# Products with the rounded activation issued on ScalarE's signal, those with the remainder on VectorE's, in a two-layer decoder on one Trainium2 core

## The reference, cut to what matters

```python
# layer 0: gated mixer, cross attention over 77 context rows, mixture of experts
xz = x @ W_in.T; xb, z = split(xz)
xc = silu(causal_conv4(xb));  proj = xc @ W_xproj.T          # B (16), C (16), delta (512)
y = (softplus(delta) * xc * sum(B * C) + D * xc) * silu(z);  mix = y @ W_out.T
att = softmax((x @ Wq) (ctx @ Wk).T / 8) (ctx @ Wv) @ Wo + bo # 16 heads of 64
moe = shared(x) + sum over the top 2 of 8 experts
# layer 1: self attention with rotary embedding (16 heads of 16), the same cross attention,
#          attention over tokens that a likeness with g_info picks
qkv = x @ W_qkv.T; att = softmax(q k.T / 4) v @ W_out.T
```

## Time and profile before

| | us |
|---|---|
| timed runs | 1549.1 and 1558.88, median 1553.99 |
| profiled execution | 1544.36 |
| its span, first to last instruction | 1542.3 |
| PE busy | 1326.4 (86%) |
| DVE busy | 979.2 (63%) |
| ACT busy | 650.5 (42%) |
| POOL busy | 423.6 (27%) |
| mean granted clock of TensorE | 0.932 of full |

### The profile page before, as it was taken

The page is one execution under the profiler, slowest core; times in us unless marked ns, Lnnn a source line. Parts: engine busy times, 40 slices in busy tenths (PEclk is TensorE's granted clock), DMA queues, the critical chain, the costliest instruction groups (busy, mean ns, idle before and its releaser), DMA issues.

```text
span 1542.3 us, 27793 instructions
## 1 busy us (share of the span) xinstructions
PE 1326.4 (86%) x11854; PEld 1097.8 (71%) x11854; DVE 979.2 (63%) x1785; ACT 650.5 (42%) x806; POOL 423.6 (27%) x405
## 2 busy tenths in 40 slices
PE   6899899998999999997699779878977957888785
PEld 6788788888878889996377558737755855556553
DVE  3676767767676446777675836666583656566573
ACT  6554556445543435652343245233414531432413
POOL 5131030210422744675034412702430240000000
PEclk9999999999999999999899899979989976978989
DMA  9361210111050316873002100200100030110000
GB/s 288 136 225 34 47 34 8 41 34 49 1 225 28 106 46 201 277 248 94 1 1 71 32 1 17 79 8 1 47 29 1 1 123 6 38 56 15 1 16 14
DMA packets 46138, 103.33 MB, mean 67 GB/s; under 512 B 4336, under 2 KB 26480, under 8 KB 45120
## 3 DMA queue, kind: packets, MB, share of 16 engines
q1 hardware_dynamic: 42944, 93.18, 18.4%
q0 software_dynamic: 3072, 8.39, 1.7%
HBM read 64.79 MB, written 36.77 MB: 66 GB/s over the span
## 4 chain that ended last, share of the span: by engine, by line
PE 68%; DVE 20%; ACT 6%; issue 3%; POOL 2%; DMA 1%; SPq 0%; POOLq 0%; DVEq 0%; ACTq 0%
PE ps L115 13%; PE ps L116 12%; PE ps L117 12%; DVE sm L1776 9%; PE ps L798 9%; PE ps L1217 4%; PE ps L1223 4%; PE ps L971 4%; PE ps L955 3%; ACT m L1639 2%; DVE m L1765 2%; DVE r L1765 2%; PE ps L1198 2%; DVE m L2192 1%; PE ps L1331 1%
## 5 line engine op out<-in xcount | busy, mean ns | idle before, releaser
L1391 ACT ACTIVATE m<-ps 128x1024 f32<-128x1024 f32 (+4 forms) x208 | 166.4, 813 | 324.7 <-PE ps L117 163.9
L1776 DVE TENSOR_REDUCE sm<-ps 128x8 f32<-128x2048 f32 (+1 forms) x128 | 193.0, 1532 | 59.0 <-PE ps L1198 34.3
L2420 POOL TENSOR_SCALAR sm<-sm 128x2 f32<-128x2 f32 x40 | 8.7, 218 | 724.1 <-DVE sm L1794 724.1
L1765 DVE TENSOR_TENSOR r<-ps,r 128x512 fp32r<-128x512 f32 (+1 forms) x159 | 116.2, 737 | 130.3 <-ACT r L1391 129.4
L1391 ACT ACTIVATE r<-ps 128x512 fp32r<-128x512 f32 (+1 forms) x159 | 100.8, 640 | 216.0 <-PE ps L798 113.6
L1639 ACT ACTIVATE m<-ps 128x2048 f32<-128x2048 f32 x64 | 119.6, 1877 | 169.2 <-PE ps L1217 169.2
L798 PE MATMUL ps<-cst,m 128*77 128x128 f32 (+1 forms) x1024 | 136.5, 277 | 21.6 <-DVE m L1765 9.4
L798 PEld LDWEIGHTS ps<-cst,m 128*77 128x77 f32 (+1 forms) x1024 | 115.0, 146 | 45.8 <-issue 17.1
L115 PE MATMUL ps<-r,w0h 128*128 128x256 f32 (+1 forms) x416 | 122.2, 294 | 16.8 <-DVE r L1765 12.5
L1198 PE MATMUL ps<-m 32*128 32x256 f32 x1024 | 103.4, 538 | 33.9 <-DVE sm L1776 30.7
L116 PE MATMUL ps<-r,w0h 128*128 128x256 f32 (+1 forms) x416 | 120.7, 290 | 0.0
(11 more groups left out here) (304 smaller groups left out, 3559.1 us busy)
## 6 DMA issues: line engine op xcount, KB each, us to landing
raw<-wu_dram SPq DMA_DIRECT2D x20, 768.0 KB, 5.6
keep_dram<-m SPq DMA_DIRECT2D x8, 768.0 KB, 3.5
m<-keep_dram SPq DMA_DIRECT2D x8, 768.0 KB, 4.3
xs_dram<-gsq SPq DMA_DIRECT2D x2, 2944.0 KB, 17.7
ys_dram<-m SPq DMA_DIRECT2D x23, 256.0 KB, 2.5
room<-wu_dram SPq DMA_DIRECT2D x7, 768.0 KB, 4.9
rt<-xs_dram SPq DMA_DIRECT2D x16, 256.0 KB, 3.2
w1raw<-w_dram SPq DMA_DIRECT2D x1, 3840.0 KB, 11.7
```

Of the source, the lines that this page charges most:

```text
L1391: return act.activation(o, i, ACT.Copy)
L1765: return dve.tensor_tensor(o, a, b_, op)
L1776: return dve.tensor_reduce(o, i, AX.X, op, **kw)
```

## The change

Two pairs of helpers split `mm3`. `whole` and `rest` are for stationary weights and a moving activation: `whole` issues the two products with the activation's rounded half, `rest` the one with the remainder. `whole_l` and `rest_l` are for a stationary activation. Each projection of a split activation waits for ScalarE's signal, issues products of `whole`, waits for VectorE's and issues those of `rest`. Where two output chunks share a bank, only one of them (chunks 0 and 2) is treated so, and the other two follow with `mm3`. The cross attention's transposed input now goes to bank 3, since its first query products, into banks 0 and 1, no longer wait for VectorE's reading of that bank. The mixer's output projection, which writes bank 2, gets a wait for VectorE's copy of the key and value products that stood there (`kv_ev[1]`). In the last sublayer `project_out` gets VectorE's signal for both. The experts keep `mm3`.

```diff
+def whole(pe, o, w, r, start):
+    pe.matmul(o, w[0], r[0], start=start, stop=False)
+    return pe.matmul(o, w[1], r[0], start=False, stop=False)
+
+def rest(pe, o, w, r, stop):
+    return pe.matmul(o, w[0], r[1], start=False, stop=stop)
+
+def whole_l(pe, o, l, w, start):
+    pe.matmul(o, l[0], w[0], start=start, stop=False)
+    return pe.matmul(o, l[0], w[1], start=False, stop=False)
+
+def rest_l(pe, o, l, w, stop):
+    return pe.matmul(o, l[1], w[0], start=False, stop=stop)
...
+                pe.wait_ge(*st.l0_act.at(b, "xT"))
+                pe.wait_ge(*w0_lo_v.at("win"))
...
+                for c in (0, 2):
+                    for k in range(2):
+                        whole(pe, into[c][0], into[c][1][k], cols(xT, A, k), k == 0)
                 pe.wait_ge(*st.l0_dve.at(b, "xT"))
...
+                for c in (0, 2):
                     for k in range(2):
-                        m = mm3(pe, st.ps[:, 1024 + c * 256:1280 + c * 256], cols(v.win, A, k, slice(c * 128, (c + 1) * 128)), cols(xT, A, k), k == 0, k == 1)
+                        rest(pe, into[c][0], into[c][1][k], cols(xT, A, k), k == 1)
+                yield
+                for c in (1, 3):
+                    for k in range(2):
+                        m = mm3(pe, into[c][0], into[c][1][k], cols(xT, A, k), k == 0, k == 1)
...
+                if 1 < b < 6:
+                    pe.wait_ge(*kv_ev[1].at(b - 2, 3))
+                for h in range(2):
+                    pe.wait_ge(*st.l0_act.at(b, f"y{h}"))
+                    for j in range(2):
+                        for k in (2 * h, 2 * h + 1):
+                            whole_l(pe, bank(st, 2 + j)[:, 0:256], cols(v.yr, A, k, slice(j * 128, (j + 1) * 128)), cols(v.wout, A, k), k == 0)
...
-                turn_x(st, b, sig)
-                yield
-                pe.wait_ge(*dve_.at(b, "xT"))
+                turn_x(st, b, sig, bank(st, 3))
+                yield
+                pe.wait_ge(*act_.at(b, "xT"))
...
                     if c % 2 == 0:
+                        pe.wait_ge(*act_.at(b, f"o{c // 2}"))
+                        for d in (c, c + 1):
+                            for j in range(2):
+                                whole_l(pe, bank(st, j)[:, 0:256], cols(v.OT, A, d, slice(j * 128, (j + 1) * 128)), cols(v.wo, A, d), d == 0)
+                    else:
                         pe.wait_ge(*dve_.at(b, f"o{c // 2}"))
...
-            def project_out(st, b, v, w, sig, dve_, o):
-                pe.wait_ge(*dve_.at(b, "oT"))
+            def project_out(st, b, v, w, sig, rounded, left, o):
+                pe.wait_ge(*rounded)
                 for j in range(2):
                     for c in range(2):
-                        m = mm3(pe, o[:, j * 256:(j + 1) * 256], cols(v.oT, A, c, slice(j * 128, (j + 1) * 128)), cols(w, A, c), c == 0, c == 1)
+                        whole_l(pe, o[:, j * 256:(j + 1) * 256], cols(v.oT, A, c, slice(j * 128, (j + 1) * 128)), cols(w, A, c), c == 0)
+                    if j == 0:
+                        pe.wait_ge(*left)
+                    for c in range(2):
+                        m = rest_l(pe, o[:, j * 256:(j + 1) * 256], cols(v.oT, A, c, slice(j * 128, (j + 1) * 128)), cols(w, A, c), c == 1)
...
-                yield from project_out(st, b, v, wfp, sig, dve_, bank(st, 2))
+                yield from project_out(st, b, v, wfp, sig, dve_.at(b, "oT"), dve_.at(b, "oT"), bank(st, 2))
```

Besides, the eleven tables of turns have other numbers, for instance:

```diff
-    "POOL": [3, 3, 3, 5, 12, 12, 12, 13, 13, 13, 13, 13, 16, 17, 18, 21, 21],
+    "POOL": [1, 4, 5, 8, 9, 11, 13, 13, 13, 13, 13, 13, 15, 16, 16, 16, 16],
```

More of the change, by code:

```diff
@@ L873, in l0 @@
                     if k % 2 == 0:
+                        pe.wait_ge(*st.l0_act.at(b, f"xr{k // 2}"))
+                    whole(pe, st.ps[0:48, 0:256], cols(v.wxp, A, k, slice(0, 48)), cols(v.xr, A, k), k == 0)
+                for k in range(4):
+                    if k % 2 == 0:
                         pe.wait_ge(*st.l0_dve.at(b, f"xr{k // 2}"))
-                    m = mm3(pe, st.ps[0:48, 0:256], cols(v.wxp, A, k, slice(0, 48)), cols(v.xr, A, k), k == 0, k == 3)
+                    m = rest(pe, st.ps[0:48, 0:256], cols(v.wxp, A, k, slice(0, 48)), cols(v.xr, A, k), k == 3)
                 m.then_inc(sig.up(b, "pB"), 1)
@@ L937, in xattn @@
                         yield
-                    for c in range(4):
-                        if c == 2:
-                            yield
+                    into = [(pair(st, i)[:, c * 256:(c + 1) * 256], [cols(v.wq, A, k, slice((4 * i + c) * 128, (4 * i + c + 1) * 128)) for k in range(2)]) for c in range(4)]
+                    for c in (0, 2):
                         for k in range(2):
-                            m = mm3(pe, pair(st, i)[:, c * 256:(c + 1) * 256], cols(v.wq, A, k, slice((4 * i + c) * 128, (4 * i + c + 1) * 128)), cols(xT, A, k), k == 0, k == 1)
+                            whole(pe, into[c][0], into[c][1][k], cols(xT, A, k), k == 0)
+                    if i == 0:
+                        pe.wait_ge(*dve_.at(b, "xT"))
+                    for c in (0, 2):
+                        for k in range(2):
+                            rest(pe, into[c][0], into[c][1][k], cols(xT, A, k), k == 1)
+                    yield
+                    for c in (1, 3):
+                        for k in range(2):
+                            m = mm3(pe, into[c][0], into[c][1][k], cols(xT, A, k), k == 0, k == 1)
                     m.then_inc(sig.up(b, f"q{i}"), 1)
@@ L1252, in a1 @@
                     pe.wait_ge(*r_dve.at("y", NT - 1))
-                yield from qkv(st, b, wao, sig, dve_, st.q_act if b >= 2 else None)
+                yield from qkv(st, b, wao, sig, act_, dve_, st.q_act if b >= 2 else None)
                 yield
@@ L1478, in xattn @@
                 act.wait_ge(*mix_dve.at(b, "ln"))
-                turned_x(st, b, xT_of(st, 3 if L else 1)[0], pe_, sig)
+                turned_x(st, b, xT_of(st, 3 if L else 1)[0], pe_, sig, bank(st, 3))
                 yield
@@ L1916, in xattn @@
                 yield
-                turned_x(st, b, xT_of(st, 3 if L else 1), act_, sig)
+                turned_x(st, b, xT_of(st, 3 if L else 1), act_, sig, bank(st, 3))
                 yield
```

46 lines of the change are left out of this document (23 added, 23 removed).

## The result

| | before | after |
|---|---|---|
| timed runs, us | 1549.1, 1558.88 | 1529.43, 1536.05 |
| median | 1553.99 | 1532.74 |
| span of the profiled execution | 1542.3 | 1534.1 |
| mean granted clock there | 0.932 | 0.921 |

The ratio is 0.9844, with a 95% interval of 0.9805 to 0.9883: 1.6% faster, inside the 2% band. The effect is real: 21 us in the first runs, 23 and 25 in the repeats.

A forecast was written before the change was run, and what follows sets the result against it. TensorE was taken to bound most of the kernel, with 28.1 us of its waits for VectorE's remainder touchable. Terms 8.8 + 3.4 + 3.8 + 1.0 = 17.0, plus 3 for the clock: 1549.1 - 20 = 1529 us, range 1507 to 1554.

The forecast's parts named there:

- One wait: A projection's first product starts on ScalarE's signal, saving 0.72 us; eight products cover VectorE's remainder.
- Layer 0, 8.8 us: Layer 0's 14 waits for VectorE's remainder, 13.6 us idle: seven save 0.72 us each, shorter ones go whole; 8.8 us.
- Queries, keys and values, 3.4 us: Layer 1's ten such waits: 0.9 us for each of three later pairs, VectorE being late next, plus 0.7; 3.4 us.
- Output projection, 3.8 us: Layer 1's output projections: eight waits save 0.47 us each, the time of four products issued ahead; 3.8 us.
- Swaps of the tables, 1.0 us: Layer 1: score block moved ahead of the transposes, and its like in cross attention; 0.2 us at 8 places, rounded to 1.
- The clock, 3 us: Layer 0: shorter stops bring fewer half-speed stretches; half of 7 us taken, less 0.5 for stretches elsewhere; 3 us.
- all three stretches named: Layer 0's half-clock stretches, behind 240.57 and near 278 and 377 us, 14 us in all, at waits the change shortens.
- All comes through (1516): Rival: the 28.1 us of idle go whole, plus 5 us of the clock's 7; 33 us, time 1516; chance 0.22.
- VectorE takes over (1541): Rival: VectorE and the layer norm replace the removed waits; 8 us gained, none from the clock, time 1541; chance 0.22.
- The second stop or load of weights (1559): Rival: each of 144 further TensorE waits costs a weight load, 27 us; net 7 to 10 slower, 1559; chance 0.08.
- Moved turns give it back (1544): Rival: moved turns in layers 0 and 1 return 12 us, with no clock gain; time 1544; chance 0.12.
- What would show it: Profile signs: remainder waits below 20 us, ScalarE's 10 to 15, layer 0 shorter by 8 to 12, layer 1 by 7 to 9.

The follow-up runs named there:

- E5: The changed kernel unaltered, run again beside the kernel before: median 1524.41 us, ratio .9851.
- E12: The changed kernel unaltered, run a third time beside the kernel before: median 1523.43 us, ratio .9852.
- E8: The changed kernel, but every projection in layer 0 waits for VectorE's signal first, leaving early starts in layer 1 only: 1538.15 us, ratio .9938.
- E4: The changed kernel with order, extra waits and tables kept, but products with the rounded half also wait for VectorE's signal: 1536.00 us, ratio .9941.
- E9: The changed kernel, but in layer 0 only the projections of x start early; those of xr, yr and OT wait for VectorE: 1526.46 us, ratio .9862.
- E7: The changed kernel, but every projection in layer 1 waits for VectorE's signal first, leaving early starts in layer 0 only: 1529.87 us, ratio .9874.
- E1: The kernel before with all eleven new tables of turns and no early starts: 1538.22 us, ratio .9952.
- E2: The changed kernel with the eleven old tables, so early starts without the new tables: 1528.34 us, ratio .9868.
- E10: The changed kernel, with the last sublayer's output projection also starting on ScalarE's signal and writing bank 3: 1520.97 us, ratio .9843.
- E3: The changed kernel with the old LAST table alone: 1519.38 us, ratio .9829.
- E6: The changed kernel with the old LAST table alone, repeated in a later job: 1522.89 us, ratio .9838.

## Why the prediction was right

The forecast was 1529 with 1507 to 1554, the measurement 1532.74, and 1523 to 1524 in the repeats. As a difference, 20 us were forecast, and 21 (first runs) to 25 (last job) measured. The largest term, layer 0, was right. The swaps of the tables were booked 3.9 us too low and the clock 3 too high; that these two cancelled is luck.

**One wait.** 0.72 us for a start on ScalarE's signal and eight products as enough cover: both as measured (1.89 to 1.17; no wait at `rest`).

**Layer 0, 8.8 us.** Right. The stage is 14.6 shorter. Its half-clock time fell from 24 to 10 us. Between E5 and E12, one kernel, 7 us of half clock in layer 0 cost 3.2 us (424.9 against 428.1); over all eight profiles with the changed layer 0 (six with 10 us, two with 17) they cost 2.6. So 14 us are worth 5 to 6 and the starts themselves 8 to 9. At one clock E8 gives 9.4. E4 and E8, without these starts, lose all of it, and E9 shows that the projections of x have most of it, as the earlier trace rows had it. One reading was off: six of the 14 waits have 1.4 to 1.9 us of idle time, not seven; the one counted as the seventh has 0.77, so the sum stands.

**Queries, keys and values, 3.4 us.** The size was too small. From the end of the layer norm behind one pair's self attention to the last ScalarE copy of the next pair's queries, where no half clock falls, there are 74.2 us before, 73.7 with the tables alone, 72.1 in the kernel after: 1.6 us for each of three pairs by the signals, where 0.9 was booked, 4.8 in sum. The step that failed is "what is late next is VectorE itself: 0.5 and 0.4 us". The remainder's waits of layer 1 do stand, shorter, at L135 (three, 0.5 us each: the four products of 512 columns don't reach over a remainder that starts late). But in the pair of the earlier trace rows TensorE's last transpose ends 20.8 us behind the layer norm instead of 22.6, while VectorE's last rotation ends only 0.9 earlier. The transposes follow TensorE's products without a stop in both, and now start (849.81) 1.6 us ahead of that rotation's end: it isn't on the path of everything behind.

**Output projection, 3.8 us.** Right. A pair has two of them. Stream 0's lies between the division and VectorE's last copy of the pair's attention output: 6.00 us in E4 and E7, 5.52 in the kernel after, E8 and E12. Stream 1's lies between that copy and the layer norm's end: 9.70 and 9.21, where no half clock falls. That is 0.48 and 0.49 a pair, 3.9 in all, the time of the four products ahead.

Together the early starts of layer 1 were booked at 7.2 us and these stretches give 8.7. At one clock E7 says 9.4, by the medians 5.5.

**Swaps of the tables, 1.0 us.** The term most mis-sized, and for a cause that isn't in the prediction. E1 gives 4.9 us by the stretches, 5.0 at one clock. The prediction put it at the score block ahead of the transposes. The exponential which that block feeds does start 0.6 us sooner behind the division (1.93 us instead of 2.55), but with the tables alone the last copy of the output comes only 0.04 sooner (6.00 instead of 6.04): in E1's first pair the exponential ends at 772.50, but the products with its result start at 773.14, behind the projection, which still waits for VectorE. What gained is a step of which the prediction says nothing: VectorE's layer norm no longer runs beside GpSimd's work, 4.2 of the 4.9 us (E1). The swap pays with the early starts only: with the old order they gain nothing before that copy (E2, 6.04), with the new one 0.48 a pair.

**The clock, 3 us.** Wrong in sum. In layer 0 half of its full price of 7 us was taken and 5 to 6 came in the first profile. But over all runs the mean clock is 0.930 before and after, so the later stages give it back, with layer 1's early starts (E7 against the kernel after, 0.937 against 0.930). Nor did all three stretches named stand behind a wait for the remainder: the one near 278 starts at 275.2, 3 us ahead of the wait at 278.19. The Trainium skill, "TensorE: Matmul & The Clock Gate", section "What's actually happening", has activity release the gate, from which I had derived that shorter stops can only help; the trace agrees for layer 0 and shows nothing of it for the whole.

**Rivals.** All comes through (1516): not reached, though layer 1 went beyond its term. VectorE takes over (1541): the first runs and repeats rule it out for the whole. In the last stage it may be so: in E10 4.0 us of TensorE's waits went and the stage kept its length, but the times at one clock leave room for a gain. The second stop or load of weights (1559): dead by E4 against E1, and by L126's spacing of 0.12 us. Moved turns give it back (1544): dead, E1 shows the tables to be a gain.

**What would show it.** Waits for the remainder 11.0 (below 20 was said), for ScalarE 11.9 (10 to 15), layer 0's half clock 10 (under 14): right, though E12, the same kernel, has 17. Layer 0 shorter by 14.6 and not 8 to 12: the clock's share. Layer 1 by 7 to 9, experts and last stage equal: not in the first profile (5.0, +3.6, +7.7), but 9.2 to 12.3 (more than was said), -0.3 to -1.2 and +0.3 to +2.7 in the repeats. I had named a last stage that moves by over 3 us through its tables as a sign of an error; E3, E5 and E6 show that the 7.7 us were not the table's.

## What to carry to other kernels

A product that needs only the first of two results can start on that result's signal; what it saved here is the distance between the two signals or the time of the products put ahead, whichever is less (0.72 us with eight products, 0.48 with four), and a further wait that is already met costs TensorE nothing measurable here (1536.0 with two, 1538.2 with one). When turns are reordered, compare each engine's durations before and after, not only who waits for whom: the largest miss here was a step of VectorE that took twice its time or more beside GpSimd's work, and no list of waits shows that. Six such steps are left in layer 0. And where the granted clock differs by stage between two profiles, repeat the profile before a stage is explained: 7 us in the last stage belonged to no edit.

## What the runs showed of the hardware

One program, with the same instructions in the same order, differs by 16 us over 11 runs (1520.09 to 1536.05) as its mean granted clock goes from 0.935 to 0.921. The stretches at 1.2 GHz come at the same kinds of places (attention, maxima, the last stage), but not in the same pairs: in the kernel after, attention's half-clock time in the pairs 1 to 4 was 13.0, 8.3, 4.1 and 2.1 us in the first profile, 8.3, 8.7, 12.6 and 3.0 in E5. The Trainium skill, "TensorE: Matmul & The Clock Gate", section "What's actually happening", calls the count of slow products at a kernel's start variable from run to run; these traces show such variation in the middle and at the end as well. What decides it from run to run, no run here shows.

VectorE's step of the layer norm (L1770, 128x256 in float32) takes 0.40 to 0.42 us where no GpSimd instruction overlaps it, and 0.81 to 1.54 where GpSimd adds to `x` or fills memory at the same time. So moving GpSimd's turns alone can shorten VectorE.
